# A state-space layer: residual rows join the output product on TensorE, mean and variance come from ScalarE's running sums, half of the step-size products run on VectorE

## The reference

```python
mu = jnp.mean(x, axis=-1, keepdims=True)
var = jnp.mean(jnp.square(x - mu), axis=-1, keepdims=True)
h = (x - mu) * jax.lax.rsqrt(var + LN_EPS) * ln_g + ln_b
xi, z = jnp.split(jnp.einsum('bld,ed->ble', h, W_in), 2, axis=-1)
xc = conv4(xi) + conv_b                      # depthwise over time, 4 taps
u = jax.nn.silu(xc)
x_dbl = jnp.einsum('bld,ed->ble', u, W_x)    # gives dt (16), Bm (16), Cm (16)
dt = jax.nn.softplus(jnp.einsum('blr,dr->bld', dt, W_dt) + b_dt)
dA = jnp.exp(jnp.einsum('bld,dn->bldn', dt, A))
dBu = jnp.einsum('bld,bln->bldn', dt * u, Bm)
hst = dA_t * hst + dBu_t                     # a scan over 512 steps
y = jnp.einsum('bdn,bn->bd', hst, C_t) + u * Dp
out = x + jnp.einsum('bld,ed->ble', y * jax.nn.silu(z), W_out)
```

## Time and profile before

| | us |
|---|---|
| median of 3 runs | 2290.22 (2289.66 to 2291.81) |
| the profiled execution | 2300.35 |
| its span | 2298.6 |
| granted clock of PE, mean | 0.909 of full speed |
| first scan of the third sublayer, last final | 1081.71, 1988.79 |

### The profile page before, as it was taken

How to read it: one execution, slowest core, us unless ns; L and a number is a source line. 1 busy time by engine, 2 the same in 40 slices (tenths; PEclk the granted TensorE clock), 3 DMA queues, 4 the chain that set the end, 5 groups by cost and what they waited for, 6 DMA issues and landing times. The chain is left out here.

```text
span 2298.6 us, 32626 instructions
## 1 busy us (share of the span) xinstructions
PE 1941.0 (84%) x9846; PEld 1136.6 (49%) x9846; DVE 1694.2 (74%) x2406; ACT 1198.6 (52%) x2466; POOL 1430.1 (62%) x1164
## 2 busy tenths in 40 slices
PE   2499999999873999947989898989898987569998
PEld 1234444444433999933444444444444433257776
DVE  4488777787744656522999999999999999655654
ACT  1066666666652433325676767676767574223222
POOL 7334435543342444422999999999999999444444
PEclk9699989898876999978999999999999999879999
DMA  3554444453143544424040404040404040101110
GB/s 81 103 110 101 103 96 108 111 124 100 51 153 127 100 70 75 76 39 157 0 148 19 148 19 148 19 148 19 148 19 148 10 148 9 60 7 37 36 36 19
DMA packets 231216, 185.57 MB, mean 81 GB/s; under 512 B 148729, under 2 KB 201601, under 8 KB 231058
## 3 DMA queue, kind: packets, MB, share of 16 engines
q1 hardware_dynamic: 216178, 162.61, 25.1%
q0 software_dynamic: 13296, 17.77, 4.4%
q10 hardware_dynamic: 1584, 3.24, 0.4%
HBM read 134.07 MB, written 49.49 MB: 80 GB/s over the span
## 5 line engine op out<-in xcount | busy, mean ns | idle before, releaser
L1769 POOL TENSOR_TENSOR mb_dbu<-mb_dtu,mb_bbc 128x1024 f32<-128x1024 f32 x256 | 600.4, 2361 | 41.8 <-DVE mb_hp L1900 29.6
L473 ACT ACTIVATE ex_plain<-at_t_ps 128x512 f32<-128x512 f32 x512 | 289.4, 595 | 185.9 <-PE at_t_ps L851 180.7
L1902 DVE TENSOR_TENSOR_SCAN mb_da_ps<-mb_da_ps,mb_dbu 128x1024 f32<-128x1024 f32 x160 | 365.3, 2283 | 12.6 <-ACT mb_da_ps L1819 12.6
L1953 PE MATMUL mb_y_ps<-mb_hc,lw_ident 128*128 128x512 f32 x640 | 323.9, 631 | 57.2 <-DVE mb_hc L1908 57.2
L610 DVE TENSOR_REDUCE at_mx<-at_s_ps 128x2 f32<-128x1024 f32 x256 | 310.8, 1219 | 51.4 <-PE at_s_ps L860 49.1
L860 PE MATMUL at_s_ps<-ex_w 48*128 48x512 f32 x512 | 228.1, 507 | 38.4 <-DVE at_mx L610 24.9
L851 PE MATMUL at_t_ps<-ex_w 64*128 64x512 f32 x512 | 221.7, 490 | 12.6 <-ACT ex_plain L473 6.7
L1953 PEld LDWEIGHTS mb_y_ps<-mb_hc,lw_ident 128*128 128x128 f32 x640 | 123.7, 199 | 215.7 <-issue 127.0
L1775 POOL TENSOR_TENSOR mb_hp<-mb_hp,mb_cbc 128x1024 f32<-128x1024 f32 x96 | 226.6, 2361 | 0.0
L1211 POOL DMA_INDIRECT x<-m_o,m_xs x71 | 113.7, 1602 | 172.8 <-DMA x<-m_o,m_xs 111.5
L1900 DVE TENSOR_TENSOR_SCAN mb_hp<-mb_da_ps,mb_dbu 128x1024 f32<-128x1024 f32 x96 | 218.8, 2279 | 2.5 <-ACT mb_da_ps L1819 2.5
(11 more groups left out here) (317 smaller groups left out, 4107.7 us busy)
## 6 DMA issues: line engine op xcount, KB each, us to landing
mb_bbc<-mb_scr SPq DMA_DIRECT2D x64, 512.0 KB, 5.4
mb_cbc<-mb_scr SPq DMA_DIRECT2D x64, 512.0 KB, 4.7
ex_w<-at_scr SPq DMA_DIRECT2D x384, 64.0 KB, 2.3
m_xs<-rt_rows SPq DMA_DIRECT2D x71, 129.0 KB
at_scr<-at_qk_hi SPq DMA_DIRECT2D x32, 256.0 KB
at_scr<-at_qk_lo SPq DMA_DIRECT2D x32, 256.0 KB
at_xin<-in_x SPq DMA_DIRECT2D x32, 128.0 KB, 2.3
ex_plain<-in_x SPq DMA_DIRECT2D x8, 512.0 KB
```

Source lines behind the costliest of these rows:

```text
L473: act.activation(probs[:, c, h, :], t_ps[:, k % 2, :], ACT.Exp, scale=SCALE).then_inc(exp_done, 1)
L1769: pool.tensor_tensor(dbu[:, q % 3, :, :], dtu_2, bbc[:, 2 * p:2 * p + 2, :], ALU.mult).then_inc(S["dbu_ready"], 1)
L1902: dve.tensor_tensor_scan(da, da, add, 0.0, ALU.mult, ALU.add).then_inc(S["scan_done"], 1)
L1953: last = pe.matmul(y_ps[:, v % 2, :], ident[:, :], src[:, j, :], start=False, stop=(q == tile_last[v] and j == 1))
```

## The change

Three edits, all in the third sublayer.

1. **Mean and variance.** DVE's `ln` is gone. ACT does it in four entries, one a block of 128 rows (slots 10 to 13): a Copy scaled by 1/256 whose running sum is the mean, a 128x1 Copy that makes -mean/16, and a Square of (x - mean)/16 whose running sum is the variance. The elementwise results go into a `res` buffer that `norm_r` overwrites later.
2. **Residual.** PE starts each of the four output groups of a batch with `ident x res` and adds the four products of W_out to it. ACT evicts the finished sum with a Copy; DVE's addition is gone.
3. **dt x u.** For even tiles DVE does it, right behind its last dt step; for odd tiles POOL does, as before, with one more wait for the product of the tile before.

```diff
 SCHEDULE (slots 10 to 13)
-    10: [("conv", 1, 1)],
-    11: [("xi", 2, 1), ("ln", 0, 2)], 12: [("xi", 3, 1)], 13: [("z", 0, 1), ("newton", 0, 2)],
+    10: [("conv", 1, 1), ("ln", 0, 2)],
+    11: [("xi", 2, 1), ("ln", 1, 2)], 12: [("xi", 3, 1), ("ln", 2, 2)], 13: [("z", 0, 1), ("ln", 3, 2), ("newton", 0, 2)],
...
 POOL
-                        if kind == "dt":
+                        if kind == "dt" and i % 2:
                             v = ND * m + i
                             emptied(pool, "dt", i, m)
                             wait(pool, S["dbu_ready"], NP * (v - 1))
+                            pool.wait_ge(S["dtu_ready"], v)
                             pool.tensor_tensor(dtu[:, i % 2, :], dt[:, i % 2, :], u[:, m % 2, i, :], ALU.mult).then_inc(S["dtu_ready"], 1)
...
 ACT
+                        if kind == "ln":
+                            act.wait_ge(S["x_loaded"], 16 * (m + 1))
+                            wait(act, S["x_stored"], 16 * (m - 2))
+                            act.activation(res[:, m % 3, i, :], xin[:, i, :], ACT.Copy, scale=1.0 / D, accum_out=mv[:, i, 0:1]).then_inc(S["stats_done"], 1)
+                            act.wait_ge(S["stats_done"], 12 * m + 3 * i + 1)
+                            act.activation(nm[:, i:i + 1], mv[:, i, 0:1], ACT.Copy, scale=-1.0 / 16.0).then_inc(S["stats_done"], 1)
+                            act.wait_ge(S["stats_done"], 12 * m + 3 * i + 2)
+                            act.activation(res[:, m % 3, i, :], xin[:, i, :], ACT.Square, scale=1.0 / 16.0, bias=nm[:, i:i + 1], accum_out=mv[:, i, 1:2]).then_inc(S["stats_done"], 1)
                         if kind == "rsqrt":
-                            act.wait_ge(S["var_ready"], m + 1)
+                            act.wait_ge(S["stats_done"], 12 * m + 12)
...
+                        if kind == "out":
+                            f, used = filled(act, "out", i, m)
+                            act.activation(res[:, m % 3, 2 * i:2 * i + 2, :], f.rearrange("p (a c) -> p a c", a=2), ACT.Copy).then_inc(used, 1)
...
 DVE
-                        if kind == "ln":
-                            dve.wait_ge(S["x_loaded"], 16 * (m + 1))
-                            wait(dve, S["h_ready"], m)
-                            for k in range(4):
-                                dve.bn_stats(stats[:, k, :], xin[:, k, :]).then_inc(S["stats_done"], 1)
-                            dve.wait_ge(S["stats_done"], 4 * m + 4)
-                            for k in range(4):
-                                last = dve.bn_aggr(mv[:, k, :], stats[:, k, :])
-                            last.then_inc(S["var_ready"], 1)
...
-                        if kind == "out":
-                            f, used = filled(dve, "out", i, m)
-                            r_2 = res[:, m % 3, 2 * i:2 * i + 2, :]
-                            dve.tensor_tensor(r_2, f.rearrange("p (a c) -> p a c", a=2), r_2, ALU.add).then_inc(used, 1)
+                            if i % 2 == 0:
+                                emptied(dve, "dt", i, m)
+                                wait(dve, S["dbu_ready"], NP * (v - 1))
+                                wait(dve, S["dtu_ready"], v)
+                                dve.tensor_tensor(dtu[:, i % 2, :], dt[:, i % 2, :], u[:, m % 2, i, :], ALU.mult).then_inc(S["dtu_ready"], 1)
...
 PE (out_a, out)
+                            pe.matmul(out[:, a * D:(a + 1) * D], ident[:, :], res[:, m % 3, 2 * i + a, :], start=True, stop=False)
                             for d in range(ND):
-                                last = pe.matmul(out[:, a * D:(a + 1) * D], u[:, m % 2, d, tok], wo[:, d, :], start=(d == 0), stop=(d == ND - 1))
+                                last = pe.matmul(out[:, a * D:(a + 1) * D], u[:, m % 2, d, tok], wo[:, d, :], start=False, stop=(d == ND - 1))
```

More of the change, by code:

```diff
@@ L1627 @@
     0: [("xi", 1, 1)], 1: [("dt", 1, 0)], 2: [("out_a", 0, -1)], 3: [("out", 0, -1)], 4: [("out_a", 1, -1)], 5: [("out", 1, -1)],
-    6: [("conv_a", 0, 1), ("final", 0, 0)], 7: [("conv", 0, 1)], 8: [("dt", 2, 0), ("load", 0, 2)], 9: [("conv_a", 1, 1)], 10: [("conv", 1, 1)],
-    11: [("xi", 2, 1), ("ln", 0, 2)], 12: [("xi", 3, 1)], 13: [("z", 0, 1), ("newton", 0, 2)], 14: [("conv_a", 2, 1), ("final", 1, 0), ("rsqrt", 0, 2)],
+    6: [("conv_a", 0, 1), ("final", 0, 0)], 7: [("conv", 0, 1)], 8: [("dt", 2, 0), ("load", 0, 2)], 9: [("conv_a", 1, 1)], 10: [("conv", 1, 1), ("ln", 0, 2)],
+    11: [("xi", 2, 1), ("ln", 1, 2)], 12: [("xi", 3, 1), ("ln", 2, 2)], 13: [("z", 0, 1), ("ln", 3, 2), ("newton", 0, 2)], 14: [("conv_a", 2, 1), ("final", 1, 0), ("rsqrt", 0, 2)],
     15: [("conv", 2, 1)], 16: [("dt", 3, 0)], 17: [("conv_a", 3, 1), ("norm_r", 0, 2)], 18: [("conv", 3, 1)], 19: [("silu_u", 0, 1)],
@@ L1652, in mamba_phase @@
         res = sb("res", [P, 3, 4, D])
-        stats, mv = sb("stats", [P, 4, 6]), sb("mv", [P, 4, 2])
+        mv, nm = sb("mv", [P, 4, 2]), sb("nm", [P, 4])
         av, lv, rs, tv, nb = (sb(q, [P, 2, 4]) for q in ("av", "lv", "rs", "tv", "nb"))
@@ L1670, in mamba_phase @@
         f_ps = ctx.enter_context(nc.psum_tensor("mb_f_ps", [P, 2, T], F32))
-        names = """prep a_exp x_stored const_set x_loaded stats_done var_ready a_made ln_done rs_ready
+        names = """prep a_exp x_stored const_set x_loaded stats_done a_made ln_done rs_ready
                    newton norm_ready h_ready f_ready hT_hi_ready z_ready u_ready scr_written ex_steps ex_ready dt_steps dtu_ready
```

## The result

The changed kernel took 2312.81 us (median of 4 runs, 2309.10 to 2317.02) beside 2291.01 us (2289.66 to 2295.81) for the kernel before: ratio 1.0092, 95% interval [1.0069, 1.0115]. It is slower by 0.9%, 21.8 us; forecast were 24.4 and 2315 us. Five more runs of the same kernel gave 1.0105 [1.0088, 1.0123].

The account below looks back on a forecast made before the run. DVE was taken as the bound, PE close behind. Terms -10.4 + 2.6 + 15.7 + 8.6 + 3.5 + 2.7 + 1.7 = +24.4 us on 2290.2 gave 2315 us, 1.1% slower; own range 2305 to 2325.

Parts of the forecast that it names:

- Statistics out of the loop, -10.4: In the loop, six batches each save DVE 1.73 us of mean and variance, hidden on ACT: -10.4 us.
- Residual, +2.6: Output groups: identity products delay PE, DVE waits 1.83 us at final 0; six batches pay +0.63, the last gains 1.2.
- the margin: At final 0 of tile 0, the slack of PE's last sum before DVE would wait: 0.23 us.
- The upper bound of +6: Residual edit in the loop: +6 us if all four identity products land on DVE.
- dt x u, slot 28, +15.7: Tile 0 of the next batch: DVE's product takes 0.73 us plus 1.5 behind POOL, seven times: +15.7 us.
- dt x u, slot 11, +8.6: Tile 2: DVE's product takes 0.73 us plus 0.35 behind POOL, eight times: +8.6 us.
- Ahead of the loop, +3.5 and +2.7: Before the loop: batch 0's statistics on ACT cost +3.5 us, batch 1's delay the last conv eviction by +2.7.
- The tail, +1.7: Behind the loop: PE's 32 records become 40, +1.7 us.
- no standing behind POOL: DVE's dt x u never stands for POOL and costs 0.73 us in both places: +11.1, 2301 us; chance 0.15.
- the running sums cost more than 1.8 us a block: ACT's statistics blocks, at 2.4 us each, add time ahead of and inside the loop: +44.0, 2334 us; chance 0.19.
- POOL sets the pace: In the loop POOL is the bound and is relieved of fifteen dt x u: -11.0, 2279 us; chance 0.08.

Follow-up runs that it names:

- final 0 one slot later: Kernel before with only the residual product on PE and ACT's eviction, and DVE's final 0 moved from slot 6 to 7: 2285.51 us, ratio 0.9968.
- edit 3 alone: Kernel before with only dt x u of even tiles moved from POOL to DVE: 2322.15 us, ratio 1.0143.
- edit 1 alone: Kernel before with only mean and variance moved to ACT's running sums, in all batches: 2282.29 us, ratio 0.9963.
- the best version: Kernel before with mean and variance on ACT for batches 2 to 7 only, DVE keeping batches 0 and 1: 2277.07 us, ratio 0.9935.

## Why the prediction was right

Step by step, forecast against measurement:

- **Statistics out of the loop, -10.4.** In this kernel DVE's wait for ACT is the same 12.1 us, so the term holds; ACT's block takes 1.27 us (the next one starts at 1247.30, the factors behind it at 1248.57), forecast 1.3. Alone the edit gives 13.85, since 3.4 us of waits vanish with it (3.0 for PE, 0.5 of DVE for its own scan); in the full change such waits are there again (2.3 at final 2, 1.4 for its own scan).
- **Residual, +2.6.** Alone +2.94 in the loop. The mechanism is the one forecast; the wait at final 0 is 1.66 us against 1.83, and a batch gets 0.54 longer by it, against 0.63 (last dt step ahead of the stretch to final 0: 16.84 us before, 17.38 after). The 0.1 lies in the way from PE to DVE: final 0 starts 0.10 us behind PE's next row (1232.31), where 0.2 had been taken, so the margin was 0.3. The upper bound of +6 doesn't come out of its own condition: four products are 1.72 us, 1.49 beyond the margin, six times that less 1.2 is +7.7. That only DVE's place in the program makes this edit a loss is shown by final 0 one slot later.
- **dt x u, slot 28, +15.7.** The seven rows (1184.58 the first, 1881.93 the last) sum to 15.6 us. POOL had 1.6 us to go, in one batch 2.1, against 1.5; behind its end dt x u took 0.55 us, where a whole 0.73 had been added. That these two cancel is luck.
- **dt x u, slot 11, +8.6.** Eight rows, 0.91 in six batches and 1.56 and 1.52 at the two ends of the loop, sum 8.5. That POOL catches up there was seen rightly: its product starts 2.00 us ahead of dt x u and has 0.36 to go, as forecast (0.35), and not the 0.96 that the earlier trace rows give directly. But in the first and the last batch it has 1.0 to go, as in most batches of edit 3 alone; the sum comes out because the six others cost less than the 1.08 forecast. That is luck too.
- **Ahead of the loop, +3.5 and +2.7.** Together +3.98 (edit 1 alone: +6.00). Batch 0's part was right, 3.27 measured from the statistics' start to rsqrt. Batch 1's delayed the last convolution eviction by 2.46, as forecast, but 1.7 us came back before the first scan. Much of that is PE's: the product that makes x_dbl took 5.46 us in place of 6.19, and two evictions of z lie 4.68 us apart in place of 5.30, with a granted clock of 0.83 between them in place of 0.54. In edit 1 alone that clock is 0.51, the distance is 5.30, and the 6.00 us stay. Why the clock differs was not tested.
- **The tail, +1.7**, was mis-sized by 1: the store is issued 1.62 us later behind the last final, but the fourth phase ends only 0.61 later.

In sum the loop was forecast at +16.5 us and came to +16.9; ahead of it 6.2 were forecast and 4.0 measured, behind it 1.7 and 0.6. What the forecast has too much lies in these two outer terms.

Of the rivals, "no standing behind POOL" fell (0.91 to 2.63 us in the loop, none at 0.69), "the running sums cost more than 1.8 us a block" fell (1.27), "POOL sets the pace" fell: POOL's waits for DVE ahead of dbu rose from 35.0 to 66.2 us. What edit 3 took from POOL became idle time: ahead of the row at 1305.91 POOL waits 2.92 us, and in the kernel before it ran dt x u and dbu there without a wait (1301.11 to 1304.82).

The rule that was weighed, the Trainium skill, SBUF — State Buffer, section "SBUF: two separate sides", holds here: of a DVE instruction with two SBUF inputs and a GpSimd instruction that reads SBUF, whichever starts first keeps the shared port pair for its whole length. The rows agree, both ways. DVE stands 1.5 us behind POOL at 1301.36 (2.18 less the 0.69 it takes alone), and POOL's product at 1241.23 takes 2.82 us in place of 2.36 while DVE's dt x u, ahead of it, finishes. The variant that reads one input from PSUM took 0.69 us beside the same work.

Not settled: why the clock fell behind three of six equal idle times in the variant without identity products, and why it was higher ahead of the loop in the changed kernel than in edit 1 alone.

## What to carry to other kernels

Before moving an elementwise product from GpSimd to VectorE, look where its inputs lie and what GpSimd runs at that moment: 0.7 us of work cost 2.2 here, and the same instruction took its 0.7 us with one input in PSUM, or one unit later. Moving work off the bound engine pays in full only until the engine next to it is reached: in the loop 13.9 us (statistics) and 9.6 us (residual, final 0 moved) alone, 11.0 together. Work that is hidden inside a loop may stand bare ahead of it; leave it there on the engine that had it, which was worth some 6 of the 13 us that the best version gains.

## What was not expected of the hardware

- An activation with a running sum leaves a second row, ACTIVATION_READ_ACCUMULATOR of 0.19 us; with the 128x1 Copy between them the two of a block take 1.27 us.
- The standing ends with a fixed step: dt x u ends 0.54 to 0.56 us behind the end of POOL's product, at slot 28 and slot 11 alike, in every run that has it. What stands costs POOL's rest and 0.55 us, not the rest and the whole 0.69.
- Less work on PE did not make it finish earlier in three of six batches: behind 1.9 us of idle time the granted clock over 5 us was 0.66, against 1.00 behind the same idle time in others.
